# A graph-attention stage: gathers without landing waits, and its row loads in slices of 16 partitions

## The reference

```python
h = (x @ W_lin + b_lin).reshape(N, HEADS, EMB)
ee = (edge_attr @ W_edge + b_edge).reshape(-1, HEADS, EMB)
x_i = h[src]
x_j = h[dst] + ee
alpha = (x_i * att_i).sum(-1) + (x_j * att_j).sum(-1)
alpha = jnp.where(alpha >= 0, alpha, NEG_SLOPE * alpha)
amax = segment_max(alpha, src)
e = jnp.exp(alpha - amax[src])
denom = segment_sum(e, src)
messages = x_j * (e / (denom[src] + 1e-16))[:, :, None]
out = segment_sum(messages, src).mean(axis=1) + bias
```

## Time and profile before

| | us |
|---|---|
| median of 2 runs (16301.63 to 16309.38) | 16305.5 |
| profiled execution | 16222.9 |
| its span, first to last instruction | 16221.2 |
| attention stage, first gather to last first score | 13140.1 to 16118.1 |

### The profile page before, as it was taken

The page is one execution under the profiler, slowest core; times in us unless marked ns, Lnnn a source line. Parts: engine busy times, 40 slices in busy tenths (PEclk is TensorE's granted clock), DMA queues, the critical chain, the costliest instruction groups (busy, mean ns, idle before and its releaser), DMA issues.

```text
span 16221.2 us, 180153 instructions
## 1 busy us (share of the span) xinstructions
PE 9592.5 (59%) x40895; PEld 6450.1 (40%) x40896; DVE 7215.4 (44%) x18628; ACT 3844.3 (24%) x8556; POOL 9525.9 (59%) x8465
## 2 busy tenths in 40 slices
PE   0466657766478878845555556655555545555555
PEld 0111122221133333335555554555555545555554
DVE  8876657777000000013333332333333357777776
ACT  0344444442011111112222222222222212222221
POOL 0378878888645434426666664566666645555553
PEclk9999999999688778865555555555555555555555
DMA  9922222222599989992222223222222344444444
GB/s 385 358 15 19 19 15 20 20 20 18 168 342 370 343 306 357 359 113 86 84 86 84 85 84 50 75 84 86 84 86 85 80 95 139 141 141 140 140 139 96
DMA packets 1483063, 2197.01 MB, mean 135 GB/s; under 512 B 882955, under 2 KB 926027, under 8 KB 1454669
## 3 DMA queue, kind: packets, MB, share of 16 engines
q1 hardware_dynamic: 907628, 1490.52, 28.2%
q0 software_dynamic: 453120, 343.50, 12.7%
q10 hardware_dynamic: 121698, 356.43, 6.0%
HBM read 1771.19 MB, written 419.98 MB: 135 GB/s over the span
## 4 chain that ended last, share of the span: by engine, by line
POOL 40%; DMA 22%; issue 21%; PE 8%; DVE 4%; another core or an unknown queue 3%; ACT 1%; POOLq 0%; SPq 0%; DVEq 0%; ACTq 0%
POOL gat L645 18%; POOL adj L613 12%; POOL arena L645 8%; DMA arena<-adj 8%; DMA gat<-q_table,ring_i 6%; DMA arena<-h_table,ring_i 5%; PE bank L1029 5%; DMA adj<-put_n,put_at 2%; POOL rec_src L599 1%; DVE arena L1356 1%; PE same L1161 1%; PE same L1000 1%; DVE arena L1358 1%; PE same L980 0%
## 5 line engine op out<-in xcount | busy, mean ns | idle before, releaser
L645 POOL DMA_INDIRECT gat<-q_table,ring_i x3456 | 3626.6, 1049 | 2405.7 <-DMA gat<-q_table,ring_i 1025.0
L613 POOL DMA_INDIRECT adj<-put_n,put_at x1632 | 2559.9, 1569 | 1265.3 <-DVE put_at L1440 638.1
L1183 PE MATMUL bank<-onehot_t,onehot 128*128 128x64 f32 x6912 | 1585.5, 424 | 2574.9 <-DVE acc L1578 1880.5
L1183 PEld LDWEIGHTS bank<-onehot_t,onehot 128*128 128x128 f32 x6912 | 1506.7, 330 | 2653.8 <-DVE acc L1578 1938.5
L599 POOL DMA_INDIRECT rec_src<-pay,ring_i x1632 | 1606.4, 984 | 1566.9 <-ACTq L743 1093.2
L645 POOL DMA_INDIRECT arena<-h_table,ring_i x1728 | 1729.4, 1001 | 1346.2 <-DMA arena<-h_table,ring_i 760.8
L1088 PE MATMUL same<-onehot 32*128 32x512 f16 x3264 | 1678.6, 615 | 620.0 <-DVE onehot L1411 389.3
L1029 PE MATMUL bank<-arena,hs 128*64 128x512 f32 x5880 | 1596.0, 707 | 508.2 <-DMA arena<-adj 506.9
L1419 DVE TENSOR_SCALAR_CACHE_REDUCE onehot<-same 128x128 bf16<-128x128 f32 (+3 forms) x1632 | 1233.0, 756 | 843.2 <-PE same L1090 675.9
L1173 PE MATMUL bank<-hs,arena 128*128 x6912 | 1564.0, 421 | 29.3 <-ACT arena L867 29.3
L1173 PEld LDWEIGHTS bank<-hs,arena 128*128 128x128 f32 x6912 | 1525.9, 333 | 29.8 <-issue 29.8
(11 more groups left out here) (277 smaller groups left out, 13003.2 us busy)
## 6 DMA issues: line engine op xcount, KB each, us to landing
arena<-adj SPq DMA_DIRECT2D x300, 2560.0 KB
arena<-rec_src SPq DMA_DIRECT2D x432, 552.0 KB
adj<-hs ACTq DMA_DIRECT2D x25, 6656.0 KB, 46.3
rec_src<-pay ACTq DMA_DIRECT2D x1, 119232.0 KB, 332.0
arena<-lo_row SPq DMA_DIRECT2D x432, 256.0 KB
hs<-b_row SPq DMA_DIRECT2D x108, 1024.0 KB
acc<-b_row SPq DMA_DIRECT2D x108, 1024.0 KB
gat<-q_table,ring_i POOLq DMA_INDIRECT x3456
```

The source lines that it names most:

```text
L613: nc.gpsimd.indirect_dma_start(counts, bass.IndirectOffsetOnAxis(put_at[:, b // 3 % 4, c:c + 1], 0), put_n[:, b // 3 % 4, c:c + 1], None, ...
L645: nc.gpsimd.indirect_dma_start(rows[n][:, u, :], None, table, bass.IndirectOffsetOnAxis(ring_i[:, n, u:u + 1], 0)).then_inc(landed[n], 16)
L1183: last = mm(bank[6 + n % 2][:, u // 2 * D:(u // 2 + 1) * D], onehot[:, n % 2, u, :], msg[n % 2][:, u, :], start=u % 2 == 0, stop=u % 2 == 1)
```

## The change

POOL's attention gathers lose the wait for the landing of the group before; the two earlier stages keep it. The place load and the broadcast become eight DMAs of 16 partitions each. The records are loaded in every fourth step for four groups at once (32 rows of 40 bytes per partition), also in eight DMAs of 16 partitions. They are asked for in step n for groups n+4 to n+7, after the weighting of group n-1. The waits of DVE and ScalarE count eight times as many arrivals.

```diff
+SPLIT = 8
+SLICE = P // SPLIT
...
             def scores(i, n):
-                if live(i, n + 7):
+                if n % 4 == 0 and live(i, n + 4):
+                    half = (n + 4) % 8 // 4
                     hold(sp, t_w, nth(i, n - 1))
-                    sp.dma_start(rec8[(n + 7) % 8], rec[:, bass.ds(i * (8 * U) + (n + 7) * U, U), 0:10])\
-                        .then_inc(t_rec[(n + 7) % 8], 16)
+                    for q in range(SPLIT):
+                        ps = slice(q * SLICE, (q + 1) * SLICE)
+                        sp.dma_start(rec_flat[ps, half * 4 * U:(half + 1) * 4 * U, :],
+                                     rec[ps, bass.ds(i * (8 * U) + (n + 4) * U, 4 * U), 0:10]).then_inc(t_rec[half], 16)
                 if live(i, n + 3):
                     hold(sp, t_m, nth(i, n - 1))
                     hold(sp, t_rel, nth(i, n - 1))
-                    sp.dma_start(lo_l3[(n + 3) % 4], lo_rows[bass.ds(i * 8 + (n + 3), 1), :].to_broadcast([P, U * P]))\
-                        .then_inc(t_lo[(n + 3) % 4], 16)
+                    for q in range(SPLIT):
+                        ps = slice(q * SLICE, (q + 1) * SLICE)
+                        sp.dma_start(lo_l3[(n + 3) % 4][ps], lo_rows[bass.ds(i * 8 + (n + 3), 1), :].to_broadcast([SLICE, U * P]))\
+                            .then_inc(t_lo[(n + 3) % 4], 16)
                 if live(i, n + 2):
...
-                    sp.dma_start(b_bc[n % 2], b_row[n % 4:n % 4 + 1].to_broadcast([P, 2 * U * P])).then_inc(t_bb[n % 2], 16)
+                    for q in range(SPLIT):
+                        ps = slice(q * SLICE, (q + 1) * SLICE)
+                        sp.dma_start(b_bc[n % 2][ps], b_row[n % 4:n % 4 + 1].to_broadcast([SLICE, 2 * U * P])).then_inc(t_bb[n % 2], 16)
...
-            def gathers(table, rows, landed, i, n, before, first):
-
-                if not first:
+            def gathers(table, rows, landed, i, n, before, free):
+
+                if not free:
                     hold(pool, landed[(n - 1) % len(landed)], i * (16 * U) + before)
...
-            def score_rows(i, n, first=False):
+            def score_rows(i, n):
                 hold(pool, t_idx, nth(i, n))
-                gathers(h_table, gat8, t_gat, i, n, (n > 0) * 16 * U, first)
+                gathers(h_table, gat8, t_gat, i, n, 0, True)
...
-                dve.wait_ge(t_rec[n % 8], i * 16 + (n // 8 * 16 + 16))
+                dve.wait_ge(t_rec[n % 8 // 4], i * (16 * SPLIT) + (n // 8 + 1) * 16 * SPLIT)
```

More of the change, by code:

```diff
@@ L170, in build @@
         aend += 2 * U * LA
+        rec_flat = arena[:, aend:aend + 8 * U * 10].rearrange("p (t r) -> p t r", r=10)
         rec8 = [arena[:, aend + n * U * 10:aend + (n + 1) * U * 10].rearrange("p (u r) -> p u r", u=U) for n in range(8)]
@@ L383, in build @@
         t_gat = [sem(f"t_gat{n}") for n in range(8)]
-        t_rec = [sem(f"t_rec{n}") for n in range(8)]
+        t_rec = [sem(f"t_rec{n}") for n in range(2)]
         t_lo = [sem(f"t_lo{n}") for n in range(4)]
@@ L659, in _ @@
                         node_rows(k, i, n)
-            def score_rows(i, n, first=False):
+            def score_rows(i, n):
                 hold(pool, t_idx, nth(i, n))
-                gathers(h_table, gat8, t_gat, i, n, (n > 0) * 16 * U, first)
+                gathers(h_table, gat8, t_gat, i, n, 0, True)
             pool.wait_ge(d_table, 16 * 3)
             for n in range(8):
-                score_rows(0, n, first=n == 0)
+                score_rows(0, n)
             with pool.Fori(1, NG // 8) as i:
@@ L920, in scores @@
                 if live(i, n + 3):
-                    done = i * 32 + ((n + 3) // 4 * 16 + 16)
+                    done = i * (32 * SPLIT) + ((n + 3) // 4 + 1) * 16 * SPLIT
                     act.wait_ge(t_lo[(n + 3) % 4], done)
@@ L1677, in mask_scores @@
             def mask_scores(i, n):
-                dve.wait_ge(t_bb[n % 2], i * 64 + (n // 2 * 16 + 16))
+                dve.wait_ge(t_bb[n % 2], i * (64 * SPLIT) + (n // 2 + 1) * 16 * SPLIT)
                 dve.wait_ge(t_abs, nth(i, n))
```

## The result

The changed kernel takes 17031.7 us (two runs, 17030.65 and 17032.83) where the kernel before took 16305.5: ratio 1.0443 [1.0413, 1.0473], slower by 726 us. That lies 132 us above the range, and the sign is that of the second rival.

The account below looks back on a forecast made before the run. It took POOL's wait for its own gathers as the bound. 7.4 + 5.1 + 0.15 = 12.65 us a group instead of 13.80, over 216 groups 248 us less, gave 16060 us; range 15780 to 16900.

Parts of the forecast that it names:

- second rival: Broadcast slices of 16 partitions are slow in themselves: 16760 if half-hidden by overlap, 17235 at full price; chance 0.25.
- The broadcast in eight DMAs: SP's broadcast in eight slices instead of one DMA: landing 5.1 us after first issue, ends 4.2 and 10.7.
- the time of the data: Within the sliced broadcast: 0.51 to 0.57 us a slice, priced from earlier narrow loads; 4.2 us taken for eight.
- L: Time from the broadcast's first issue to its landing: 4.3 us as one DMA, 5.1 us in eight slices.
- the base: Attention step of the kernel before, from which the saving was counted: 13.80 us a group, 216 groups.
- What would show it: Signs: DVE's wait before masking, SP's issue spacing (0.41 us, wider for the slow-slice case), time from first issue to masking.
- The frame: POOL's gather wait goes and DVE waits for the broadcast; wrong if DVE still waits for gathers or POOL stays limiting.
- No landing wait: POOL no longer waits for its gathers: 3.5 us off its group; about 11 us a group if nothing else came up.
- What is late next: After POOL's wait goes, the broadcast's chain sets the step: 7.4 us plus its landing time, 11.7 as one DMA.
- the circle of the broadcast: DVE's masking, maximum, ScalarE's copy, SP's store, broadcast, next masking: 7.4 us from masking to issue, plus landing time.
- The places: Place load in eight DMAs: seven more issues, 2.9 us of SP a step, costing nothing unless they delay the next store.
- The records: Records for four groups in eight DMAs: 4 us of issue, store late 0.5 us once in four steps, 0.15 a step.

Follow-up runs that it names:

- e7: e1 with the broadcast in two DMAs of neighbouring halves, partitions 0 to 63 and 64 to 127: 16378.3 us.
- e8: e1 with the broadcast in two DMAs, even partitions and odd partitions: 16005.1 us.
- e3: The changed kernel with each of the eight broadcast DMAs going to every eighth partition instead of 16 neighbouring ones: 16551.7 us.
- e1: The kernel before with only POOL's landing wait for its attention gathers removed; broadcast, places and records stay one DMA each: 15977.6 us.
- e6: e1 with only the records changed, loaded for four groups in eight DMAs of 16 partitions: ratio 0.9752 to the kernel before.
- e12: The kernel before, unchanged, run once more for its profile: ratio 1.0004, 14.52 us a group.

## Why the prediction was wrong

**The step that failed is *The broadcast in eight DMAs*, in it the time of the data.** I gave a slice of 128 KB 0.51 to 0.57 us, at 62 to 70 engine-us per MB, "since the quiet load is the nearer row", and L = 5.1. Eight slices of 16 neighbouring partitions cost 125 engine-us per MB and L = 10.4. In the terms of its sum, 0.8 + 4.2 + 0.1: the start was 1.0, the data 7.9, and from the last data to the masking 1.6 us. The row was near in one respect (13 partitions, same queue) and far in the one that counts: its six DMAs carried 52 KB each at the pace of their issue, so they hardly queued behind each other; that this is why their packets were cheap is argued and not shown. The same rows gave a second reading, 107 GB/s. I called it a lower bound because of that pace, and it was one, though a near one: the data moved at 135 GB/s.

**The mechanism is the second rival's**, and its full price was nearly right: L = 10.7, 18.1 us, 17235 worked out; 10.4, 17.80 us, 17031.7 measured. There is luck in that: 9.8 us of data and 0.1 behind it stood for 7.9 and 1.6, and the time came out 200 us too high because of the base (below). Wrong was to halve it "by overlap of neighbouring slices" and to end the range there. No row spoke for the overlap, and with L = 8.5 worked out and 10.4 measured there was little of it. The runs show the locality (e7 against e8, e3 against the changed kernel) and not why it is so. The Trainium skill, SBUF — State Buffer, Door 1, gives 104 GB/s for 1 MiB into partitions 0 to 15 and says that partitions 0 to 63 reach half of the ports. The order agrees with these runs, 79 against 52 engine-us per MB in halves and 135 GB/s in the changed kernel, which is above the figure of the Trainium skill; here eight slices follow each other and not one transfer alone. By that page of the Trainium skill, which sends partitions four by four to the ports, even and odd partitions reach them all, which fits e8. The Trainium skill, DMA: Bandwidth & Descriptors, Rules for kernel authors, which the prediction named first, gives another reason against a split, that the parts serialize on the same engines. That reason holds as well for even and odd partitions, which cost 0.3 us a group; so it is not what cost 5 us here.

**What would show it** had three numbers for this rival. Two came: DVE's wait of "5 or more" is 7.1, and "8 to 11 us" from first issue to masking is 10.4. The third did not come where I looked for it: the eight issues kept their 0.44 us. The queue takes all eight, and it is the records' issues behind them that stand 1.0 us apart.

**The frame held.** *No landing wait* is worth 359 us alone (e1), and POOL's wait moved to the indices. *What is late next*, the circle of the broadcast, set the step in e1 and in the changed kernel: 7.25 + 5.5 and 7.3 + 10.5 us on the mean of 180 groups, and in both DVE stands before the masking until the broadcast has landed. One size in it was off. L of a single DMA is 5.2 and not 4.3: I had ended it at the fall of the traffic and not at the start of the masking. The 7.4 from masking to issue was right.

**The places** I priced at nothing; by difference they cost 77 us against e1 and more against e6. **The records** I priced at 0.15 us a group, for a store that is late once in four steps. Beside a whole broadcast they cost nothing (e6); in the changed kernel the store is 0.85 us late in every fourth step, 0.2 us a group, so the size of the term was about right, though its issues took 7.8 us and not 4.

**The base.** The sum started from a step of 13.80 where the profile at the median time has 14.52 (e12). With that and the circle's 12.65 I would have said 404 us less instead of 248: the error of the base has nothing to do with the sign. The second rival's 18.1 us would have given 17079 instead of 17235, 47 from the 17031.7 that came.

## What to carry to other kernels

When a wait is removed, draw the next circle with each of its terms before pricing the rest of the change. Here it had 2 us to spare at most, and the change put 5 us into it; moving one copy ahead took 2.3 us out and gave 4.4% together with the first part. A broadcast like this one is issued whole; if it must be sliced, then with its partitions interleaved and in few slices. And a rate read from transfers that never queued is no price for transfers that do: if the rows bound a cost from both sides, the range goes to the end and not to the middle.

## What the runs showed of the hardware

- A MB of SP's loads costs 52 engine-us when the broadcast goes to all partitions or every second one, 69 with every eighth, 79 with halves, 111 to 125 with sixteen neighbours. These are means with the records and places, and in the runs with 69 and 125 the places are sliced too. One row of 8 KB of the broadcast takes 0.31, 0.45, 0.61 and 0.89 to 1.02 us (medians).
- SP issues slices of neighbouring partitions 0.44 us apart and slices of every eighth partition 0.62 us apart. Behind eight slow slices the next eight issues stand 1.0 us apart (7.79 us in the changed kernel).
- Traffic, data and landing differ. In e1 the whole broadcast was issued at 14609.29; the traffic from 14609 to 14619 (slices of 0.25 us) falls from its plateau at about 14613.2, the last packet of the broadcast ends at 14613.97, and the masking starts at 14614.52:

```profile
GB/s 100 0 0 0 50 232 148 328 360 459 393 393 393 393 492 295 334 142 218 256 238 312 305 116 83 200 67 0 0 0 33 200 34 0 0 67 200 0 0 0
```
